# Experts on their own tokens: rows sorted by expert into fifteen tiles, in place of all experts on all tokens

## The reference

```python
        rprobs = jax.nn.softmax(logits.astype(jnp.float32), axis=-1)
        topw, topi = jax.lax.top_k(rprobs, TOPK)
        topw = topw / jnp.sum(topw, axis=-1, keepdims=True)
        wfull = jnp.zeros((T, E), jnp.float32).at[jnp.arange(T)[:, None], topi].set(topw)
        out = jnp.zeros((T, HID), h.dtype)
        for e in range(E):
            w1 = w13[e, :FFN]
            w3 = w13[e, FFN:]
            g = jax.nn.silu(h @ w1.T) * (h @ w3.T)
            out = out + jnp.einsum('tf,hf->th', g, w2[e]) * wfull[:, e:e + 1]
        return x + out.reshape(B, S, HID)
```

## Time and profile before

| | us |
|---|---|
| median of three executions | 2225.64 |
| the profiled execution | 2225.48 |
| its span, first to last instruction | 2223.7 |
| PE busy | 1614.2 |
| DVE busy | 1626.8 |
| ACT busy | 1174.6 |
| POOL busy | 1233.7 |

### The profile page before, as it was taken

The page is one execution under the profiler, slowest core; times in us unless marked ns, Lnnn a source line. Parts: engine busy times, 40 slices in busy tenths (PEclk is TensorE's granted clock), DMA queues, the critical chain, the costliest instruction groups (busy, mean ns, idle before and its releaser), DMA issues.

```text
span 2223.7 us, 29267 instructions
## 1 busy us (share of the span) xinstructions
PE 1614.2 (73%) x7664; PEld 938.7 (42%) x7664; DVE 1626.8 (73%) x2538; ACT 1174.6 (53%) x1906; POOL 1233.7 (55%) x1097
## 2 busy tenths in 40 slices
PE   3677676766677666765376887877879888897888
PEld 1445454544455444544133343443434434343443
DVE  3999999999999999996262738456384654837455
ACT  4565555656565555561146391754727357282751
POOL 2777677777777677774336280643717346181541
PEclk8888777877888777775567598898989989899999
DMA  4212022121212011120301000000100001000000
GB/s 149 82 77 84 21 82 81 76 95 76 95 76 91 21 74 81 76 91 12 115 6 36 11 27 11 16 35 16 36 8 9 34 16 36 16 10 26 11 0 15
DMA packets 39620, 107.23 MB, mean 48 GB/s; under 512 B 4128, under 2 KB 30048, under 8 KB 34368
## 3 DMA queue, kind: packets, MB, share of 16 engines
q1 hardware_dynamic: 39520, 106.24, 12.6%
HBM read 92.99 MB, written 8.65 MB: 46 GB/s over the span
## 4 chain that ended last, share of the span: by engine, by line
issue 25%; POOL 13%; PE 6%; DVE 4%; DMA 2%; ACT 1%; SPq 0%; POOLq 0%; DVEq 0%; ACTq 0%
POOL pp L1892 9%; DMA k<-k_scratch 1%; DVE mx L1583 1%; PE pbk L1224 1%; PE po L1231 1%; PE pa L1218 1%; PE og L1167 1%; PE scores L1119 1%; PE scores L1117 1%; POOL ln_r L1822 0%; DVE rec L1611 0%; POOL kp L1855 0%; ACT pt L1414 0%; POOL rotk L1851 0%; PE scores L1147 0%
## 5 line engine op out<-in xcount | busy, mean ns | idle before, releaser
L731 POOL TENSOR_TENSOR hc<-hb,cb 128x512 f32<-128x512 f32 x512 | 653.8, 1295 | 249.3 <-DVE hb L610 221.4
L610 DVE TENSOR_TENSOR_SCAN hb<-da,dbu 128x512 f32<-128x512 f32 x512 | 599.5, 1202 | 5.6 <-DVE stats L635 4.0
L499 ACT ACTIVATE da<-dt,a_neg 128x512 f32<-128x512 f32 x512 | 351.9, 717 | 352.9 <-DVE hb L610 303.9
L331 PE MATMUL yp<-ident,hc 128*128 128x128 f32 x2048 | 359.0, 317 | 65.0 <-POOL hc L731 64.6
L1892 POOL TENSOR_TENSOR pp<-pt,pp 128x512 f16<-128x512 f32 x320 | 365.0, 1151 | 71.7 <-ACT pt L1414 71.3
L331 PEld LDWEIGHTS yp<-ident,hc 128*128 128x128 f32 x2048 | 297.9, 166 | 174.3 <-POOL hc L731 93.2
L603 DVE TENSOR_TENSOR dbu<-dtu,bp 128x512 f32<-128x512 f32 x512 | 323.8, 677 | 4.0 <-PE bp L319 3.2
L1583 DVE TENSOR_REDUCE mx<-scores 128x1 f32<-128x384 f32 (+3 forms) x352 | 218.4, 636 | 131.0 <-PE scores L1119 127.9
L1693 DVE SCALAR_TENSOR_TENSOR ga<-th,pa 128x512 f32<-128x512 f32 x128 | 87.6, 685 | 246.4 <-ACT th L1429 246.4
L1413 ACT ACTIVATE pp<-scores,lift 128x512 f16<-128x512 f32 x320 | 221.5, 692 | 46.3 <-PE scores L1147 45.4
L319 PE MATMUL bp<-st,sel 96*128 96x512 bf16 x256 | 116.4, 455 | 151.7 <-DVE dbu L603 149.0
(11 more groups left out here) (181 smaller groups left out, 2265.6 us busy)
## 6 DMA issues: line engine op xcount, KB each, us to landing
cb<-c_scratch SPq DMA_DIRECT2D x16, 3072.0 KB, 11.8
cb<-c_scratch SPq DMA_DIRECT2D x16, 1024.0 KB, 4.6
q<-q_scratch SPq DMA_DIRECT2D x24, 288.0 KB
q_scratch<-qp SPq DMA_DIRECT2D x24, 128.0 KB
q<-q_scratch SPq DMA_DIRECT2D x24, 96.0 KB
xin<-in_x SPq DMA_DIRECT2D x8, 256.0 KB, 11.5
xres<-xin SPq DMA_DIRECT2D x8, 256.0 KB, 2.4
xres<-xln SPq DMA_DIRECT2D x8, 256.0 KB, 2.6
```

The costliest lines, as they stand in the source:

```text
L331: last = nc.tensor.matmul(yp[:, c, h * P:(h + 1) * P], src[:, c * P:(c + 1) * P], ident[:, :], is_transpose=True, start=(s < 0 and h == 0 ...
L499: nc.scalar.activation(da[:, s % NDA, :], dt[:, d, h, :], ACT.Exp, scale=a_neg[:, d, h, n:n + 1]).then_inc(da_done, 1)
L610: nc.vector.tensor_tensor_scan(hb[:, s % NHB, :], da[:, s % NDA, :], dbu[:, s % 2, :], 0.0, ALU.mult, ALU.add).then_inc(scan_done, 1)
L731: nc.gpsimd.tensor_tensor(hc[:, s % NHC, :], hb[:, s % NHB, :], cb[:, d, s // 2, :], ALU.mult).then_inc(hc_done, 1)
```

## The change

The tokens of a sequence are no longer sent through every expert. After the gate, each token's two (token, expert) pairs get a slot number: the pairs are counted per expert with matmuls against a triangular and an all-ones matrix (`pe_count`), each expert starts at a new tile of 128 slots, and 512 x 2 pairs with eight experts need at most fifteen tiles (`NT` = 15, `NSLOT` = 1920). `dve_gate` grows from 12 to 27 steps, in the turn at t = 19 and on. POOL scatters the normalised rows `h2n` into a scratch tensor `xs` by eight indirect DMAs of 128 rows; SP reads `xs` back as `xg` in sorted order (960 KB); TensorE transposes it, VectorE copies it to `xt` with the norm's weight. The number of the expert of each tile is read from SBUF into a register of SP, and the tile's own weights (128 x 768 float32, 384 KB) are loaded from HBM into one of eight buffers `wt`: fifteen loads a sequence.

The MoE then runs over four groups of four tiles (the last of three): each a, w3 and w2 step is four calls of 128 columns with four sets of weights, while tanh, ga and g take the four tiles in one operation. The result has tokens on partitions (`ysb`), goes to a scratch tensor `ys`, and is gathered by eight more indirect DMAs in the next turn (`pool_gather`); eight VectorE operations at the start of the main after that add the two weighted rows and x2e. The weight of an expert is thus applied at the end, and the broadcast of weights (L1211), `h2e` and the final transposition are gone. All twenty MoE slots lie in main, at t = 9 to 37; none is left in the turn. The end part (statistics, POOL's normalisation, store) moves from the turn to the main stage of the round after, POOL's share at t = 5. SP's order in a round is written out anew in `sp_round`. Once, at the start, `xs` is filled with zeros.

```diff
+NT = TC * TOP + NE - 1
+GT = 4
+NG = -(-NT // GT)
...
+GATHER_SLOTS = {6: 0, 8: 1, 17: 2, 25: 3}
+MOE_SLOTS = {9 + 3 * k // 2: k for k in range(5 * NG)}
+
+
+def tiles(q):
+
+    return range(GT * q, min(GT * (q + 1), NT))
...
+        def sp_xg(sp, b):
+            written = count.in_register(sp, scattered, b, 16 * TC * TOP)
+            taken = count.in_register(sp, xg_ready, b, 0)
+            sp.wait_ge(scattered, written)
+            sp.wait_ge(xg_ready, taken)
+            sp.dma_start(xg[:, :, :], xs.rearrange("(j p) m -> p j m", p=P)).then_inc(xg_loaded, 16)
+
+        def sp_w(sp, b, q):
+
+            chosen_by = count.in_register(sp, gate_step, b, 24)
+            used = count.in_register(sp, down_done, b, NF * (q - 1))
+            sp.wait_ge(zeroed, 16)
+            sp.wait_ge(gate_step, chosen_by)
+            sp.wait_ge(down_done, used)
+            for j in tiles(q):
+                e = sp.value_load(exp_i[0:1, j:j + 1], min_val=0, max_val=NE - 1)
+                sp.dma_start(wt[:, j % NWT, :].unsqueeze(1), w["w_e"][bass.ds(e, 1)].rearrange("a p n -> p a n")
+                             ).then_inc(w_loaded[q], 16)
+
+        def sp_y(sp, b, q):
+            made = count.in_register(sp, y_out, b, q + 1)
+            taken = None if is_first(b) else count.in_register(sp, gathered, b - 1, 16 * TC * TOP)
+            sp.wait_ge(y_out, made)
+            if taken is not None:
+                sp.wait_ge(gathered, taken)
+            j0, j1 = tiles(q)[0], tiles(q)[-1] + 1
+            sp.dma_start(ys[j0 * P:j1 * P].rearrange("(j p) m -> p j m", p=P), ysb[:, j0:j1]).then_inc(y_stored[q], 16)
...
+        def sp_round(sp, b):
+
+            later = not isinstance(b, int) or b + 1 < NB
+            sp_w(sp, b - 1, 0)
+            sp_w(sp, b - 1, 1)
+            sp_xg(sp, b - 1)
+            if later:
+                sp_xa(sp, b + 1)
+            if not isinstance(b, int) or b > 1:
+                sp_xr(sp, b - 2)
+                sp_out(sp, b - 2)
+            sp_y(sp, b - 1, 0)
+            sp_w(sp, b - 1, 2)
+            if later:
+                sp_parts_out(sp, b + 1)
+            sp_w(sp, b - 1, 3)
+            sp_y(sp, b - 1, 1)
+            if later:
+                sp_parts_in(sp, b + 1, 0)
+            sp_y(sp, b - 1, 2)
+            if later:
+                sp_parts_in(sp, b + 1, 1)
+            sp_y(sp, b - 1, 3)
+            if later:
+                sp_max(sp, b + 1)
...
             sp_max(sp, 0)
+            sp.wait_ge(consts, 5)
+            sp.dma_start(xs.rearrange("(j p) m -> p j m", p=P), xg[:, :, :]).then_inc(zeroed, 16)
             sp_xa(sp, 1)
...
+        def pe_a(pe, b, q, f):
+            n = NF * q + f
+            if f == 0:
+                pe.wait_ge(w_loaded[q], count(w_loaded[q], b, 16 * len(tiles(q))))
             pe.wait_ge(ga_done, count(ga_done, b, n))
-            if n == 0:
-                pe.wait_ge(moe_in, count(moe_in, b, 1))
-            nc.tensor.matmul(pa[:, :], w13[:, e, f * P:(f + 1) * P], h2t[:, :],
-                             start=True, stop=True).then_inc(a_ready, 1)
...
+            pe.wait_ge(xt_done, count(xt_done, b, q + 1))
+            for i, j in enumerate(tiles(q)):
+                last = nc.tensor.matmul(pa[:, i * P:(i + 1) * P], wt[:, j % NWT, f * P:(f + 1) * P], xt[:, j * P:(j + 1) * P],
+                                        start=True, stop=True)
+            last.then_inc(a_ready, 1)
...
         def pe_main(pe, att=None, moe=None, front=None):
-            if moe is not None:
-                for slot in range(EARLY_SLOTS):
-                    pe_moe(pe, moe, slot)
             for t in range(ST_TILES):
                 if att is not None:
                     pe_st(pe, att, t)
-                if moe is not None and t in MAIN_SLOTS:
-                    pe_moe(pe, moe, MAIN_SLOTS[t])
+                if moe is not None:
+                    if t in GATHER_SLOTS:
+                        pe_xg(pe, moe, GATHER_SLOTS[t])
+                    if t in MOE_SLOTS:
+                        pe_moe(pe, moe, MOE_SLOTS[t])
...
+        def dve_keep(dve, b):
+
+            dve.wait_ge(gate_step, count(gate_step, b, GATE_STEPS))
+            if not is_first(b):
+                dve.wait_ge(gathered, count(gathered, b - 1, 16 * TC * TOP))
+            nc.vector.tensor_copy(pos_e[:, :, :], posi[:, :, :]).then_inc(keep_done, 1)
+            dve.wait_ge(ye_done, count(ye_done, b, 0))
+            nc.vector.tensor_copy(wn_e[:, :, :], wn[:, :, :]).then_inc(keep_done, 1)
+
+        def dve_xt(dve, b, q):
+            dve.wait_ge(xg_ready, count(xg_ready, b, q + 1))
+            dve.wait_ge(b_ready, count(b_ready, b, NF * (q + 1) - NG * NF))
+            n = len(tiles(q)) * P
+            nc.vector.tensor_scalar(xt[:, q * SEQ:q * SEQ + n], m1[:, 0:n], lnw[:, 1:2], None,
+                                    ALU.mult).then_inc(xt_done, 1)
...
         def dve_end(dve, b, k):
             if k == 0:
-                dve.wait_ge(ot_ready, count(ot_ready, b, 1))
+                dve.wait_ge(gathered, count(gathered, b, 16 * TC * TOP))
+                dve.wait_ge(keep_done, count(keep_done, b, 2))
                 dve.wait_ge(out_done, count(out_done, b, 0))
-                dve.wait_ge(moe_in, count(moe_in, b, 3))
+                dve.wait_ge(x2_kept, count(x2_kept, b, 1))
                 dve.wait_ge(end_step, count(end_step, b, 0))
-                nc.vector.tensor_tensor(ye[:, :, :], m1[:, :].rearrange("p (c m) -> p c m", c=TC), x2e[:, :, :],
-                                        ALU.add).then_inc(ye_done, 1)
+                for j in range(TOP):
+                    for c in range(TC):
+                        if j:
+                            dve.wait_ge(ye_done, count(ye_done, b, c + 1))
+                        nc.vector.scalar_tensor_tensor(ye[:, c, :], yk[:, c, j, :], wn_e[:, c, j:j + 1],
+                                                       ye[:, c, :] if j else x2e[:, c, :],
+                                                       ALU.mult, ALU.add).then_inc(ye_done, 1)
...
+        def dve_main(dve, att=None, moe=None, front=None, end=None):
+            if end is not None:
+                dve_end(dve, end, 0)
             if moe is not None:
-                dve_h2e(dve, moe, 0)
-            for slot in range(EARLY_SLOTS):
-
-                if front is not None and slot == EARLY_SLOTS - 1:
+                dve_keep(dve, moe)
+            if front is not None:
+                dve_in(dve, front, 0)
+            if end is not None:
+                if front is not None:
                     dve.wait_ge(in_step, count(in_step, front, 4))
-                if moe is not None:
-                    dve_moe(dve, moe, slot)
-                if front is not None and slot >= EARLY_SLOTS - 2:
-                    dve_in(dve, front, slot - EARLY_SLOTS + 2)
+                dve_end(dve, end, 1)
+            elif front is not None:
+                dve.wait_ge(in_step, count(in_step, front, 4))
+            if front is not None:
+                dve_in(dve, front, 1)
+            elif end is not None:
+                dve.wait_ge(end_step, count(end_step, end, 4))
+                dve_end(dve, end, 2)
             for t in range(ST_TILES):
 
                 if att is not None and t in (14, 24, 34):
                     dve_og(dve, att, (t - 14) // 10)
-                if moe is not None and t in MAIN_SLOTS:
-                    dve_moe(dve, moe, MAIN_SLOTS[t])
+                if moe is not None:
+                    if t in GATHER_SLOTS:
+                        dve_xt(dve, moe, GATHER_SLOTS[t])
+                    if t in MOE_SLOTS:
+                        dve_moe(dve, moe, MOE_SLOTS[t])
                 if front is not None:
+                    if t == 1 and end is not None:
+                        dve.wait_ge(end_step, count(end_step, end, 4))
                     if t in (1, 4):
                         dve_in(dve, front, {1: 2, 4: 3}[t])
+                    if t == 1 and end is not None:
+                        dve_end(dve, end, 2)
...
-                    if 19 <= t < 31:
+                    if t >= 19:
                         dve_gate(dve, post, t - 19)
-                    if t in (37, 39):
-                        dve_wpart(dve, post, (t - 37) // 2)
+            if post is not None:
+                dve_gate(dve, post, GATE_STEPS - 2)
+                dve_gate(dve, post, GATE_STEPS - 1)
...
+        def pool_scatter(pool, b):
+            placed = count.in_register(pool, gate_step, b, 20)
+            taken = count.in_register(pool, xg_loaded, b, 0)
+            pool.wait_ge(zeroed, 16)
+            pool.wait_ge(gate_step, placed)
+            pool.wait_ge(xg_loaded, taken)
+            for c in range(TC):
+                for j in range(TOP):
+                    nc.gpsimd.indirect_dma_start(xs[:, :], bass.IndirectOffsetOnAxis(ap=posi[:, c, j:j + 1], axis=0),
```

(45 more changed lines are left out.)

480 lines of the change are left out of this document (241 added, 239 removed).

## The result

The changed kernel takes 2403.12 us (median of 4 runs, 2400.34 to 2404.87), the kernel before 2224.24 us beside it on the same chip: ratio 1.0802, 95% interval 1.0774 to 1.0830. The forecast was 2313 us with a range of 2205 to 2400. The direction was right, the size was not: +179 us where +87 had been worked out, 3 us beyond the range. The profiled execution has a span of 2400.3 us, against 2223.7 before, so the two traces together have 176.6 us to explain.

What follows compares the result with a forecast made beforehand. Three waits bound main: POOL's late start, its list, the parts' DMA out and in. 2225.5 + 60 (rounds 2 to 6) + 9 (round 1) + 6.5 (round 0) + 12 (last main, tail) = 2313 us; range 2205 to 2400.

Steps and rivals of the forecast that it cites:

- Start of main: Round start to POOL's first split: 21 us instead of 11.7 (+9.3), xa following eight weight loads and xg.
- The list: POOL's splits and parts in main, with the end's normalisation: 43.8 + 4.6 - 3.4 = 45 us (bounds 42 and 49).
- The parts: Parts out to the turn's first matmul: 22.9 becomes 28 us, with weight loads and the y1 store between.
- The turn: Turn without MoE: round 0's 49.9 us plus 3.5 for gate steps and counting, 53.4 us; -3.5 a round.
- Last main and tail: Last main +5.5 us, PE waiting for xg; tail from 70.0 to 76.5 us, +6.5; together +12.
- Round 0: First round: zero-fill of 960 KB ahead of xa +3 us, gate +3.5; +6.5 us.
- (a): Rival, faster: six tiles ready ahead in main pay for the late start; 2215 us; chance 0.17.
- (b): Rival, it cancels: main's steps and the turn each near their good end, +0.5 us a round; 2235 us; chance 0.13.
- (c): Rival: POOL's indirect DMAs take 4.2 us each, delaying main's start; about 2430 us, 2370 at 2.8 each; chance 0.14.
- (d): Rival: TensorE's MoE passes of 128 columns cost 0.21 us instead of 0.11; 2390 us; chance 0.08.

Runs made afterwards that it cites:

- e4: Changed kernel with the fifteen weight loads taking a fixed expert instead of one read from SBUF into a register; 2367.9 us, ratio 1.0651.
- e5: Changed kernel with twelve weight buffers; SP issues xa, xr, xg first, then three groups' weights, the fourth's after the y0 store, ahead of the parts; 2257.0 us.
- e12: e9 and e10 together, plus sixty idle matmuls ahead of the tail's wait for xg; 2185.9 us, ratio 0.9816.
- e3: Changed kernel with twelve weight buffers instead of eight: third group's weights loaded at round start, fourth's behind the y0 store, ahead of the parts; 2367.8 us.
- e7: Changed kernel with the gate's token counting in bf16 and in eight matmuls instead of 22 small passes; 2388.6 us, ratio 1.0744.
- e11: Changed kernel with two idle bf16 matmuls of 256 columns behind each step of the turns; 2383.4 us, ratio 1.0697.
- e6: e5 with the gate's token counting in bf16 and in eight matmuls instead of 22 small passes; 2221.8 us, ratio 0.9986.
- e9: e6 with two idle bf16 matmuls of 256 columns behind each step of the turns; 2192.2 us, ratio 0.9842.
- e10: e6 with the second sequence's xa ahead of the zero-fill, and DVE's weighted sums in the last main held until the scatter has ended; 2204.8 us.
- e8: Changed kernel with DVE's weighted sums in the last two mains held until the scatter has ended; 2419.7 us, one run.
- e2: Changed kernel without the rounds' weight loads, the eight buffers filled once before the first round; 2272.5 us, ratio 1.0225.

## Why the prediction was wrong, step by step

- **Start of main: 21, measured 24.3.** The mechanism was right (SP: eight loads, xg, xa). Eight issues took 8.55 us, not 9.6; xa landed 20.0 us in, not 16.8. Too small was the data: with the eight loads ahead xg took 8.2 us to land instead of the 5.2 I gave it, xa 8.7 instead of 2.9, and its issue alone held SP for 4.3. The register read, for which I took 0.6, is 0.53 (e4). The Trainium skill, page DMA: Bandwidth & Descriptors, section Latency and other measured facts, has a floor of about 600 ns for it; e4's 0.53 us is close to it, slightly below.
- **The list: 45, measured 47.3**, 46.5 wherever TensorE had no late rows or weights. Of the 4.6 us of end operations on POOL 1.6 were hidden (46.5 against 43.5 before), where I had counted 3.4. Round 1, which has no end operations, has a list of 50.5, and still 49 to 52 in e5 to e12, though its POOL has less to do. I had made it shorter. These are 9 of round 1's 13 us. No run tests them, but the rows show a path that I had not counted. DVE, PE, POOL in order of time, main of round 1:

```profile
1294.29 4.52 DVE L1600 TENSOR_SCALAR hn<-xa,mv,ln_r 128x128 f32<-128x128 f32 x4
```

```profile
1299.62 1.09 PE L1302 MATMUL m<-ident,xg 128*128 128x128 f32 x4 [2.89 <-DVE xt L1783]
```

```profile
1303.59 1.16 POOL L2007 TENSOR_TENSOR pp<-pt,pp 128x512 f16<-128x512 f32 x1 [3.75 <-ACT pt L1486]
```

Nine splits run there without a gap, and DVE's hn beside them takes 4.5 us, where in round 2, with the end's normalisation among the splits, it takes 2.5. So xt, behind it on DVE, comes later, TensorE waits 2.9 us for it (1.8 in round 2), and the next scores, and with them POOL, come late.

- **The parts: 28, measured 30.0.** Here the step itself failed, and the number was near by luck. I counted w(3) as 3.6 us of issue between parts out and parts in and named the turn's first matmul as the one who waits. I did not ask who waits for w(2) and w(3): TensorE, in order, with the scores of the next tiles behind it. Four more loads behind y0 and three behind the parts: I had taken the MoE's 20 us on TensorE as work without a transfer to wait for. The turn's first matmul, for whose DMA I had added 5 us, waits for none in the changed kernel; what stands in their place is 7.3 us of TensorE's waits for w(2) and w(3). e3, which has these loads earlier, gives 22.7, near the 22.3 of before.
- **The turn: 53.4, measured 53.4**, and both parts of the reason were off. The MoE's absence gave what round 0 showed, the counting took 4.3 (e7 against the changed kernel), the DVE steps nothing that shows. "I let the clock stay at 0.53" was right as a forecast and hid what the change gives away: the MoE had kept the turn at 0.86, and a clock of 0.74 to 0.86 is worth about 2 us a turn, 3.4 at best (e11, e12).
- **Last main and tail: +12, measured +49.** The last main missed by 12: TensorE waits for xg, behind eight loads, and for weights (e5, with xg first, has 88.1). The tail missed by 25: 17 of it are the same unasked question (44.4 us of MoE; 27.1 in e3, without the waits), 3 the size of the steps (27 against the 24 counted), 3.6 the scatter (15.0 against 11.4, with the pause of 2.2 and the wait for the last landing). Gates 10.0 against 9.3, xg 5.7, gather 11.4 against 11.4 and the end 9 were right.
- **Round 0: +6.5**, measured +6.5: zero-fill 3.2 and counting.

The rivals. (a), the head start pays, decides below start + list = 61: 71.6 in the changed kernel, 57 in e5, e6, e9, e10 and e12, whose mains are about as long as before (79.8 against 79.1). So its condition was the right one, and it was the order on SP that kept it away; its 2215 us needed a turn of 50.5 and a tail of 76.5 beside, which e5 did not have (56.2, with the pause, and 84.0). In the sums of (a) and (b) the 6.5 us of the tail and those of round 0 are added once, not twice, and the last main's 5.5 not at all; with them they are 2227 and 2247 us. (c), dear indirect DMAs: no. 121 of 128 take 0.94 to 1.09 us, mostly 1.25 to 1.28 from one to the next, six 1.17 to 1.45, one 3.54, against the 1.15 taken; the scatter ends 3.4 us into the round, on the tenth as forecast. (d), 128 columns don't gain: no. A call of four tiles takes 1.05 us for its eight passes, as the earlier trace rows; about 1.9 at half clock.

The range ended at 2400, since the 0.08 above it had one cause, the indirect DMAs. What came was a cause that I had not listed.

## What to carry to other kernels

A load added to an in-order queue has two prices: what it delays behind it, and who waits for it where it stands. Ask both for each load, and of every buffer, from which moment it is free; two groups of weights behind a store and behind the parts cost nearly as much here (7 us a round and 14 in the tail) as all eight in front (9 us a round). Put what the slowest chain starts with first, then the rows with the earliest consumer, then weights in the order of use: that and three small repairs made of a change that loses 8% one that gains 1.8%. And when work leaves a stage, look at what else it was doing there: TensorE's idle stage fell to half clock, and DVE, which waits for its matmuls, paid about 2 us of 53. Last, before a difference between two runs is put down to an edit, look where in the stage it lies: 13 to 15 us of four runs here lie in one pause, and in e8 at least no edit made it.

## What the runs showed of the hardware that I had not expected

- Idle matmuls made a stage shorter. At a granted clock of 0.52 (1.2 GHz for all but its start) the turn of round 3 took 49.1 us (e10), at 0.86 (2.4 GHz for most of it) 45.7 (e12). In e12's turn DVE is busy for 38.8 of the 45.7 us, so there is little left to win in it.
- DVE stood idle for 0.5 to 2.4 us at one place of the turn, with the scores that it waits for ready, in four runs on one chip and in none of the others. The cause is open.
- With DVE's two-input sums beside it, one of POOL's indirect DMAs took 2.90 to 3.54 us in ten kernels, and at most 1.43 where the sums were held back (e8, e10, e12). The Trainium skill, page SBUF — State Buffer, section Who interferes with whom, has two-input operations contend only with GpSimd's reads and infers that descriptor writing is not among them. This place speaks against the inference, round 2 for it (1.17 and 1.01 us beside the same eight sums). What tells the two apart is open.
- A transfer's issue blocks SP when enough is queued ahead: xa's took 0.4 us before, 0.6 behind the 960 KB alone (e2) and 4.3 behind these and eight loads of 384 KB.
- The landing of the scatter depends on the weights beside it: xg could be issued at 4.7 us without loads (e2) and at 8.4 with them (e4), the scatter having ended 3.4 us into the round both times.
